# Attention scores of four heads in one run over six PSUM banks, with transposes written back into them

## What is computed

```python
q = (layernorm(x) @ Wq.T + bq)      # 16 heads of 32
k = (ctx @ Wk.T + bk)               # 722 rows per batch
v = (ctx @ Wv.T + bv)
scores = einsum('bhnd,bhtd->bhnt', q, k) / sqrt(32) + mask
out = einsum('bhnt,bhtd->bhnd', softmax(scores), v)
x = x + tanh(g_xattn) * (out @ Wo.T + bo)
x = x + tanh(g_ffn) * experts(layernorm(x))   # top 2 of 8 experts, three layers with gelu
```

## Time and profile before

| | |
|---|---|
| three runs | 1771.19, 1772.03, 1772.13 us, median 1772.03 |
| span of the profiled execution | 1769.9 us, 2.1 below the median of the runs |
| PE busy | 1751.8 us, 99% of the span |
| DVE, ACT, POOL busy | 1241.7 (70%), 953.6 (54%), 182.7 (10%) us |
| granted TensorE clock | 0.998 of full speed |
| attention, batches 1 to 14 | one body every 60.5 to 60.6 us |

### The profile page before, as it was taken

The page is one execution under the profiler, slowest core; times in us unless marked ns, Lnnn a source line. Parts: engine busy times, 40 slices in busy tenths (PEclk is TensorE's granted clock), DMA queues, the critical chain, the costliest instruction groups (busy, mean ns, idle before and its releaser), DMA issues.

```text
span 1769.9 us, 39880 instructions
## 1 busy us (share of the span) xinstructions
PE 1751.8 (99%) x14694; PEld 1517.9 (86%) x14694; DVE 1241.7 (70%) x3382; ACT 953.6 (54%) x1780; POOL 182.7 (10%) x271
## 2 busy tenths in 40 slices
PE   9999999999999999999999999999999999999997
PEld 8888888888888888888888877877899999999996
DVE  5677787778778777877776556666677777777772
ACT  4655656565555556565655544545555555545551
POOL 1110110111011001100100010010000100101010
PEclk9999999999999999999999999999999999999999
DMA  8982222222122222222204299999766666776661
GB/s 264 381 316 69 80 86 69 72 80 83 53 79 85 66 66 81 86 69 71 76 29 156 94 334 395 364 350 296 218 208 209 205 208 208 217 219 219 219 196 36
DMA packets 123230, 292.68 MB, mean 165 GB/s; under 512 B 17860, under 2 KB 36292, under 8 KB 123089
## 3 DMA queue, kind: packets, MB, share of 16 engines
q1 hardware_dynamic: 99664, 225.46, 38.1%
q0 software_dynamic: 23424, 65.30, 12.7%
HBM read 244.04 MB, written 46.66 MB: 164 GB/s over the span
## 4 chain that ended last, share of the span: by engine, by line
PE 86%; DMA 2%; DVE 2%; issue 1%; ACT 0%; SPq 0%; POOL 0%; DVEq 0%; ACTq 0%; POOLq 0%
PE bank_rows L2366 21%; PE bank_rows L727 13%; PE bank_rows L713 12%; PE bank_rows L775 7%; PE bank_rows L2381 6%; PE bank_rows L765 4%; PE bank_rows L2420 4%; PE bank_rows L786 4%; PE bank_rows L2447 3%; PE bank_rows L2406 3%; PE bank_rows L802 2%; DMA stage<-in_L_ffn_w 2%; PE bank_rows L750 2%; PE bank_rows L851 1%; PE bank_rows L865 1%; PE bank_rows L789 1%
## 5 line engine op out<-in xcount | busy, mean ns | idle before, releaser
L1177 ACT ACTIVATE probs<-probs,neg_max 100x722 f32<-100x722 f32 x248 | 221.0, 892 | 107.8 <-DVE neg_max L1528 107.8
L1521 DVE CUSTOM_DVE_ANT_0 probs<-bank_rows,mask_sb 100x362 f32<-100x362 f32 x496 | 234.4, 529 | 8.0 <-PE bank_rows L765 7.1
L2610 DVE TENSOR_TENSOR w_low<-stage,w_high 128x1024 fp32r<-128x1024 f32 x176 | 212.8, 1222 | 35.4 <-ACT w_high L2514 35.0
L1182 ACT ACTIVATE p_t<-bank_rows 121x600 f32<-121x600 f32 x256 | 171.3, 669 | 69.0 <-PE bank_rows L775 67.0
L2514 ACT ACTIVATE w_high<-stage 128x1024 fp32r<-128x1024 f32 x176 | 183.6, 1056 | 34.1 <-DMA stage<-in_L_ffn_w 33.9
L2537 ACT ACTIVATE gelu<-bank_rows,biases 128x256 f32<-128x256 f32 x176 | 82.1, 472 | 220.8 <-PE bank_rows L2366 197.2
L2366 PE MATMUL bank_rows<-h_low,w_high 128*128 128x256 f32 x704 | 199.2, 283 | 0.0
L2366 PE MATMUL bank_rows<-h_high,w_low 128*128 128x256 f32 x704 | 199.2, 283 | 0.0
L2366 PE MATMUL bank_rows<-h_high,w_high 128*128 128x256 f32 x704 | 199.2, 283 | 0.0
L713 PE MATMUL bank_rows<-ctx_high,wk_high 128*128 128x360 f32 (+1 forms) x512 | 182.5, 356 | 0.6 <-DVE ctx_low L1487 0.4
L775 PE MATMUL bank_rows<-ident,probs 100*121 100x100 f32 x1488 | 180.6, 257 | 1.2 <-ACT p_t L1182 1.0
(11 more groups left out here) (250 smaller groups left out, 3836.0 us busy)
## 6 DMA issues: line engine op xcount, KB each, us to landing
stage<-in_L_ffn_w SPq DMA_DIRECT2D x240, 512.0 KB, 4.4
plain_w<-in_L_ffn_w SPq DMA_DIRECT2D x15, 2048.0 KB, 11.9
expert_in_rows<-filling POOLq DMA_DIRECT2D x8, 3341.0 KB, 20.9
router_rows<-in_gate_rows POOLq DMA_DIRECT2D x112, 200.0 KB, 3.4
ctx_raw<-in_ctx SPq DMA_DIRECT2D x16, 720.0 KB, 4.4
ctx_raw<-in_ctx SPq DMA_DIRECT2D x15, 724.0 KB, 4.3
xs_sb<-expert_in_rows SPq DMA_DIRECT2D x11, 514.0 KB, 5.3
b_sb<-in_L_ffn_b SPq DMA_DIRECT2D x19, 256.0 KB
```

The lines of the kernel that those rows point to most:

```text
L1177: nc.scalar.activation(p, p, ACT.Exp, bias=neg_max[:, h:h + 1], scale=-1.0, accum_out=exp_sum[:, h:h + 1]).then_inc(probs_ready, 1)
L1182: nc.scalar.activation(p_t[:, h % HQ, :, :].rearrange("t (k i) s -> t k (i s)", k=2), bank_rows[0:TT, 4:6, 0:3 * S], ACT.Copy).then_inc(pt ...
L1521: nc.vector.tensor_tensor_reduce(out=probs_of(b, g)[:, q, at], in0=score_bank[q][0:S, 0:size], in1=mask_sb[:, at], scale=-1.0, scalar=BIG, ...
L2610: nc.vector.tensor_tensor(lo, src, hi.bitcast(F32), ALU.subtract).then_inc(chunk_lo[which], 1)
```

## The change

The six PSUM banks 0 to 5 become twelve slots of 256 columns, three for each head of a group. The 722 columns of the context are taken in three pieces of 242 columns that start 240 apart, so two columns between pieces are computed twice; the mask holds a value there that keeps the repeated ones from counting. `scores(b, g)` is now one run of 36 products of 242 columns (nine steps of four heads) with no other work between. Because heads 0 and 1 share bank 1, and heads 2 and 3 bank 4, the pieces go in an order that never lets two heads write one bank at a time, and heads 1 and 3 wait once for heads 0 and 2 (`even_piece_done`).

There are no banks for transposes left: `transpose_probs(b, pair)` writes two heads' transposes into the slots that their scores had, and ACT copies two heads at a time (1200 columns). The next `scores` must wait until the last copy of the group is done. DVE takes out one head with one instruction over 726 columns; the join of two extremes (64 instructions) is gone, and an exponential waits for its own head only. `scored_around` puts `scale_o` between the third and the fourth head.

The orders of all bodies are written anew: `attend` of the group before follows directly on each `scores`, `K31` moves behind `A0`, and the two exceptions in `SAME_BANK` go. An odd body differs from an even one as before (`Q23` after `A0`, `K10` and `K00` later). In the last body the second score buffer of SBUF (`more_probs`) is gone too. The mask comes in two DMAs instead of one.

```diff
+PIECES, PIECE, PIECE_STEP, SLOT = 3, 242, 240, 256
+TWICE = PIECE - PIECE_STEP
+PIECE_ORDER = ((2, 0, 1), (1, 2, 0))
...
-EVEN_BODY = ("K31", "A3", "V3", "Y", "V4",
-             "V5", "V0", "A0", "K00", "K10",
-             "XT", "K20", "A1", "V1", "K01", "K11",
-             "K30", "CNT", "A2", "Q01", "V2", "K21")
+EVEN_BODY = ("A3", "V3", "Y", "V4", "V5",
+             "A0", "K31", "V0", "K00", "K10",
+             "A1", "XT", "K20", "V1", "K01", "K11",
+             "A2", "K30", "CNT", "Q01", "V2", "K21")
...
-SAME_BANK = {("CNT", "A2"), ("XT", "A2")}
...
-    score_bank, pt_bank, unit_bank = banks[0:4], banks[4:6], banks[6:8] + banks[0:2]
+    unit_bank = banks[6:8] + banks[0:2]
+    slots = bank_rows[:, 0:6, :].rearrange("p b n -> p (b n)").rearrange("p (k n) -> p k n", n=SLOT)
...
-            pool.wait_ge(scored, 11 * e // 2 + 1)
+            pool.wait_ge(scored, 11 * e // 4 + 1)
...
+        def load_mask(n):
+            src = batch_rows(mask, n)
+            sp.dma_start(pieces(mask_sb[:])[:, :, TWICE:],
+                         src[:, TWICE:T].rearrange("s (k t) -> s k t", k=PIECES)).then_inc(mask_loaded, 16)
+            sp.dma_start(mask_sb[:, 0:TWICE], src[:, 0:TWICE]).then_inc(mask_loaded, 16)
...
-        def scores(b, g, half):
-            after_unit(b if (g, half) == (DT - 1, 1) else b - 1, f"K{g}{half}")
-            if half == 0:
-                after_unit(*query_unit(b, g))
-            if g > 0 or half > 0 or b > 0:
-                pe.wait_ge(scored, 2 * H * b + 2 * HQ * g + HQ * half)
-            off, size = HALVES[half]
-            for step, (a, c) in enumerate(PRODUCTS):
-                for q in range(HQ):
-                    rows = slice(q * HD, (q + 1) * HD)
-                    last = nc.tensor.matmul(score_bank[q][0:S, 0:size], q_t[a][rows, g, slot(b), :],
-                                            k_hl[c][rows, g, off:off + size],
-                                            start=(step == 0), stop=(step == 2))
+        def scores(b, g):
+            for half in range(2):
+                after_unit(b if (g, half) == (DT - 1, 1) else b - 1, f"K{g}{half}")
+            after_unit(*query_unit(b, g))
+            if g > 0 or b > 0:
+                pe.wait_ge(pt_copied, PAIRS * (DT * b + g))
+            for turn in range(PIECES):
+                for step, (a, c) in enumerate(PRODUCTS):
+                    for q in range(HQ):
+                        rows = slice(q * HD, (q + 1) * HD)
+                        k = PIECE_ORDER[q % 2][turn]
+                        if (turn, step) == (PIECES - 1, 0) and q % 2 == 1:
+                            pe.wait_ge(even_piece_done, HQ // 2 * (DT * b + g) + q // 2 + 1)
+                        last = nc.tensor.matmul(slots_of(q)[0:S, k, 0:PIECE], q_t[a][rows, g, slot(b), :],
+                                                k_hl[c][rows, g, k * PIECE_STEP:k * PIECE_STEP + PIECE],
+                                                start=(step == 0), stop=(step == 2))
+                        if (turn, step) == (0, 2) and q % 2 == 0:
+                            last.then_inc(even_piece_done, 1)
             last.then_inc(scores_ready, 1)
...
-        def transpose_probs(b, h):
-            pe.wait_ge(probs_ready, H * b + h + 1)
-            if H * b + h > 0:
-                pe.wait_ge(pt_copied, H * b + h)
...
+        def transpose_probs(b, pair):
+            pe.wait_ge(probs_ready, H * b + 2 * pair + 2)
+            for q in range(2 * pair % HQ, 2 * pair % HQ + 2):
+                for i, (off, rows) in enumerate(TILES):
+                    off += TWICE * (i // 2)
+                    last = nc.tensor.transpose(slots_of(q)[0:rows, i // 2, i % 2 * S:(i % 2 + 1) * S],
+                                               probs[:, q, off:off + rows], ident[0:S, 0:S])
             last.then_inc(pt_ready, 1)
...
         def exps(b, h):
-            if h % HQ == 0:
-                act.wait_ge(max_ready, DT * b + h // HQ + 1)
-            p = probs_of(b, h // HQ)[:, h % HQ, :]
+            act.wait_ge(scored, H * b + h + 1)
+            p = probs[:, h % HQ, :]
...
+        def copy_probs(b, pair):
+            act.wait_ge(pt_ready, H // 2 * b + pair + 1)
+            q = 2 * pair % HQ
+            nc.scalar.activation(p_t[:, q:q + 2, :, :].rearrange("t q (k i) s -> t (q k) (i s)", k=PIECES),
+                                 slots[0:TT, PIECES * q:PIECES * (q + 2), 0:2 * S],
+                                 ACT.Copy).then_inc(pt_copied, 1)
...
-        def score(b, g, half):
...
+        def score(b, g, qs=range(HQ)):
+
+            if qs[0] == 0:
+                dve.wait_ge(scores_ready, DT * b + g + 1)
+                held()
+            for q in qs:
                 h = HQ * g + q
                 nc.vector.tensor_tensor_reduce(
-                    out=probs_of(b, g)[:, q, at], in0=score_bank[q][0:S, 0:size], in1=mask_sb[:, at],
+                    out=pieces(probs[:, q, :]), in0=slots_of(q)[0:S, :, 0:PIECE], in1=pieces(mask_sb[:]),
                     scale=-1.0, scalar=BIG, op0=ALU.add, op1=ALU.min,
-                    accum_out=half_max[:, half, h:h + 1]).then_inc(scored, 1)
-            if half == 1:
-                dve.wait_ge(scored, 2 * H * b + 2 * HQ * (g + 1))
-                at = slice(HQ * g, HQ * (g + 1))
-                nc.vector.tensor_tensor(neg_max[:, at], half_max[:, 0, at], half_max[:, 1, at],
-                                        ALU.min).then_inc(max_ready, 1)
+                    accum_out=neg_max[:, h:h + 1]).then_inc(scored, 1)
+
+        def scored_around(b, g, body, of, at):
+
+            score(b, g, range(HQ - 1))
+            scale_o(body, of, at)
+            score(b, g, (HQ - 1,))
```

More of the change, by code:

```diff
@@ L474, in attention, with pieces, slots_of @@
     row_at = table("row_at", [1, PLACES + NSMALL])
-    def probs_of(b, g):
-        return more_probs if b == B - 1 and g % 2 == 1 else probs
+    def pieces(ap):
+        return ap.rearrange("s (k t) -> s k t", k=PIECES)
+    def slots_of(q):
+        return slots[:, PIECES * q:PIECES * (q + 1), :]
     def query_places(body, name, m):
@@ L875, in first_body @@
             b, n = 0, 1
-            scores(b, 0, 0)
-            keys(b, b, 3, 1)
-            scores(b, 0, 1)
+            scores(b, 0)
             values(b, 3)
@@ L895, in first_body @@
+            transpose_probs(b, 2)
+            keys(b, n, 0, 0, BACK)
+            transpose_xn(b, 1, "XS")
+            values(b, 1, FRONT)
+            transpose_probs(b, 3)
+            values(b, 1, BACK)
+            scores(b, 2)
+            attend(b, b, 0, 1)
+            keys(b, n, 1, 0)
+            values(b, 2, FRONT)
             transpose_probs(b, 4)
-            keys(b, n, 0, 0, FRONT)
+            values(b, 2, BACK)
+            keys(b, n, 2, 0)
             transpose_probs(b, 5)
-            keys(b, n, 0, 0, BACK)
@@ L915, in first_body @@
-            keys(b, n, 0, 1, BACK)
-            scores(b, 3, 0)
+            keys(b, n, 0, 1)
+            scores(b, 3)
+            attend(b, b, 0, 2)
             keys(b, n, 3, 0)
             transpose_xn(b, 2)
[L920 to L927, removed]
@@ L962, in body @@
                 keys(b, n, 0, 0)
-                transpose_probs(b, 5)
-                keys(b, n, 1, 0, FRONT)
-                transpose_probs(b, 6)
-                keys(b, n, 1, 0, BACK)
-            transpose_probs(b, 7)
-            scores(b, 2, 0)
+                transpose_probs(b, 3)
+                keys(b, n, 1, 0)
+            scores(b, 2)
+            attend(b, b, odd, 1)
             if b + 2 < B:
@@ L972, in body @@
             keys(b, n, 2, 0)
[L973 to L976 removed]
+            values(b, 1, FRONT)
+            transpose_probs(b, 4)
+            values(b, 1, BACK)
             keys(b, n, *((1, 0) if odd else (0, 1)))
[L978 to L983 removed]
@@ L985, in body @@
-            scores(b, 3, 0)
+            transpose_probs(b, 5)
+            keys(b, n, 0 if odd else 1, 1)
+            scores(b, 3)
+            attend(b, b, odd, 2)
             keys(b, n, 3, 0)
             count_pairs(b, t)
-            scores(b, 3, 1)
-            attend(b, b, odd, 2)
             if odd:
-                values(b, 2)
-                transpose_probs(b, 12)
+                values(b, 2, FRONT)
+                transpose_probs(b, 6)
+                values(b, 2, BACK)
                 keys(b, n, 1, 1)
-                transpose_probs(b, 13)
+                transpose_probs(b, 7)
@@ L1089, in on_tensor @@
         for _ in range(RUN_UP):
-            nc.tensor.matmul(score_bank[3][:, 0:P], ident[:], ident[:], start=True, stop=True)
+            nc.tensor.matmul(unit_bank[1][:, 0:P], ident[:], ident[:], start=True, stop=True)
         pe.wait_ge(pt_zero, 1)
@@ L1320, in body @@
+            recip_copy(b, 2)
+            exps(b, 13)
             keys_high(b, n, 3, 0)
-            recip_copy(b, 2)
-            exps(b, 12)
-            exps(b, 13)
-            if not odd:
-                queries_high(b, "Q01" if b < B - 2 else "Q")
```

(8 more changed lines are left out.)

473 lines of the change are left out of this document (192 added, 281 removed).

## The result

| | before | after |
|---|---|---|
| runs, median | 1771.85 us (4 runs, 1771.19 to 1772.13) | 1803.49 us (1798.32, 1803.24, 1803.73, 1809.31) |
| ratio | | 1.0181, 95% interval 1.0169 to 1.0192 |
| span of the profiled execution | 1769.9 us | 1796.6 us |
| mean granted clock of those runs | 0.998 | 0.994, 0.991, 0.992, 0.988 |
| PE busy | 1751.8 us | 1731.5 us |

The account below looks back on a forecast made before the run. It took PE's own stream as the bound, 60.5 us per body. Bodies 1 to 13 +8.5, body 14 and the start of batch 15 -1, body 0 -0.4, batch 15 +2.5: +9.6, median 1781.5 us, range 1767 to 1798.

Parts of the forecast that it names:

- wait A: Group 2: `K20` needs the bank of `A1`, emptied by DVE behind three heads; 1.7 in even bodies, 1.3 in odd ones.
- wait B: Group 3: `Q01` or `V2` needs the bank of `K30`, emptied by DVE behind four heads; PE waits 1.5.
- shorter stream: PE's pieces shrink by 2.1 per body and waits for half a group's scoring by 0.2; in sum 2.3 us.
- body 0: Two waits behind `K00` and `K30`, 3.2, against 2.0 saved and three stops of 1.6 it had: -0.4.
- body 14 and batch 15: Body 14 has no `XT` and a stop goes: -1; batch 15 has 5.8 of waits, 1.5 before, saves 1.9: +2.5.
- The scores' run: Each group's nine steps at 0.111 plus 0.175 take 1.17 instead of 1.34, saving 0.17 per group, 0.68 per body.
- DVE's head: DVE's scoring of one head of 726 columns takes 0.84, four 3.35; bounds 0.46 and 0.92.
- the stop of 2.6 in batch 15: `early_transpose(1)` waits for DVE's copy, ready 4.5 after the scores, while PE is there at 1.85: 2.6.
- The rival of short steps that columns don't bound: In scores, a step stays at 0.165 (+31) or becomes 0.26 (over +80) instead of 0.11; 10%, mostly for a partial loss.
- the stop ahead of `K31`: At the start of batch 15, a stop of 1.4 (941.57 to 942.97) goes, now covered by whole scores.
- The mask's second DMA: It and POOL's threshold come 10 us and more ahead of their users.
- DVE is 0.6 late for group 2: In even bodies DVE's 13.8 of work exceeds PE's 13.5 in group 1, so its group 2 scoring starts 0.6 late.

Follow-up runs that it names:

- a_only: The change with `XT` and its ACT copy moved ahead of `A1` in bodies 1 to 13; 1790.81 us, 1.0110 of before.
- b_only: The change with the counts (`CNT`, with place, carry and aim) behind the last transposes in bodies 1 to 14; 1772.95 us, 1.0008 of before.
- split_late: The change with the two instructions splitting `o_t` put behind the key's low half on DVE, group 3, bodies 1 to 14; 1785.77 us, 1.0081 of before.
- ab: The change with both `XT` ahead of `A1` and the counts behind the last transposes; 1755.19 us, 0.9910 of before; again 1753.20, 0.9901.
- a_longer: The change with `o_t` behind all four heads of scoring instead of three, in all groups; 1839.21 us, 1.0381 of before.

## Why the prediction was right in sign and wrong in size

The profiled spans differ by 26.7, forecast 9.6:

| term | forecast | measured |
|---|---|---|
| waits A and B, bodies 1 to 13 | +39.0 | 13 x (1.27 + 1.63) = +37.7 |
| shorter stream, bodies 1 to 13 | 13 x 2.35 = -30.5 | 13 x 1.95 = -25.3 |
| half clock there | 0 | 3 x 1.7 = +5.1 |
| rest of these bodies | 0 | +1.7 |
| body 0 | -0.4 | -0.2 |
| body 14 and batch 15 | +1.5 | +7.1 (one low stretch in it) |
| behind attention | 0 | +0.6 |

(The forecast's 3.0 less 2.3 is 0.7 and not 0.65; its sum uses 0.65, and so a saving of 2.35.)

**Right.** The scores' run (1.17 forecast, 1.19 measured), DVE's head (0.84 and 0.83), the place, number and nearly the size of both waits (1.5 and 1.5 forecast, 1.27 and 1.63 measured), the stop of 2.6 in batch 15, nothing for `even_piece_done` and, in the bodies, nothing for the next scores on the last copy. The rival of short steps that columns don't bound is out: a step is 0.11. The Trainium skill, "TensorE: Matmul & The Clock Gate", Part 3, "The mechanism", lets a load of weights overlap a product only where the row groups differ; read as I did, that asked for 0.26. The same section also lets a load go ahead into a background weight buffer, which I had left out. The rows show 0.11, with the next step's loads lying over the products of this one:

```profile
684.57 0.17 PEld L778 LDWEIGHTS bank_rows<-k_low,q_high 32*100 32x100 f32 x4
684.68 0.17 PEld L778 LDWEIGHTS bank_rows<-k_high,q_low 32*100 32x100 f32 x4
```

The first step's products, in the timeline above, run from 684.48 for 0.36.

**Wrong, in order of size.**
1. *"Bodies 1 to 13: 3.0 of waits less 2.3 = +0.65 each, +8.5."* This is the step that failed: a wait was priced by its own length. One of 1.6 also takes, in 12 of 28 cases (the change and `a_only`), 1.7 of half clock behind it. That is 7 us in the profiled run and by the clocks some 12 in the median one, the largest part of the miss. No row of before had such a wait in the bodies, so nothing there priced it; as a rival it was missing altogether. `b_only` takes away wait B and `split_late` shortens it, and in both no low stretch is left in bodies 1 to 14 and the clock is back at 0.996.
2. *"In sum 2.3 us per body."* The stream got shorter by 1.95. Counted as the forecast counts, each piece from the end of the one before, over bodies 1 to 13 of before and of `ab`: scores 0.64 (forecast 0.68), keys and values 0.82 (0.88), transposes 0.43 (0.35 and 0.15), waits 0.12 (0.2), and the queries cost 0.07 more (nothing). So no single term failed; nearly every one is a little short. The price of a key or value tile behind scores was right: a key tile takes 2.19 there before, and 2.01 behind an attention product in `ab`. +5, 0.6 of it from the 2.35 in the sum.
3. *"the stop ahead of `K31` at the start of batch 15 goes (941.57 to 942.97, 1.4"* and *"It has 1.5 now"*, for batch 15. Between the two rows lie six transposes and a half of scores, which is work and not a stop; the waits that the trace of before names between 900 and 1000 us are none. Batch 15 has its forecast stops (5.3 of 5.8), but next to nothing was saved against them: +4 with body 14.
4. *"The mask's second DMA and POOL's threshold lie 10 us and more ahead of their users."* From batch 2 on DVE never waits for the mask. In batch 1 it waits 2.58 for it, and PE then 1.5. The mask is issued at 83.0, its 300 packets of the first DMA end at 93.9 and the 100 of the second at 95.7, 1.6 behind the time at which DVE comes for it. Body 0 was still even, so this hid in other terms.
5. *"DVE is 0.6 late for group 2"* (even bodies). DVE begins 0.2 behind the end of the scores in all bodies, which the forecast's 0.2 for semaphores already holds, and wait A is 1.27 and not 1.5. Wait B is 1.63 and not 1.5, so over 13 bodies the two together are only 1.3 under the forecast.

I had said that pieces over 1.3, a head under 0.75 or less than 25 us of waits would make me wrong. None of them came, and the time lay outside the range all the same: the list tested the terms I had, not the one I lacked.

## What to carry over

Where two banks take turns, ask of each short tile whether the tiles on both sides of it share a bank whose emptying stands behind long work. Moving the short tile cost nothing here, and two such moves were worth 2.7%, turning a loss of 1.8% into a gain of 0.9%. Price a new wait on PE by its length and by what the clock does behind it, and prefer two short waits well apart to one long one.

## What the runs showed of the hardware

- The granted clock fell to 1.2 GHz for 3.4 us behind waits of PE of 1.56 us and more, not each time: behind 12 of 28 of 1.63 (the change, `a_only`), 7 of 13 of 2.1 (`a_longer`), and never behind the 39 of 1.27 (the change, `b_only`, `split_late`). It also fell behind 6 of 14 pairs of waits of 0.6 to 1.2 and 0.8 within 2.6 us (`a_longer`). Why it falls behind one such wait and not the next, no run here shows. The runs of one kernel differ with it: 11 us among four runs of the change (clock 0.994 to 0.988), 1 among those of before (0.998).
- Products of 32 x 242, four heads at a time in the four row groups, follow each other at 0.11 us a step, against 0.17 for 362 columns; loads of 0.16 to 0.17 us lie over them.
- The mask's 282 KB took 3.6 us in 100 packets of 2888 bytes and 6.6 to 6.8 in 300 packets of 960, in both cases beside the filling of the expert rows.
- One DVE instruction of 726 columns costs 0.83 from start to start, two of about 362 cost 0.92: the columns count, and joining them saves 0.09.
